# Three of eight one-hot columns of the sorting loop move from VectorE to ScalarE

## The reference

```
edge_index = jnp.stack([src, dst])
x = x + _L0_gnn_ref(_layernorm(x, axis=-1), edge_index, L0_gnn_W, L0_gnn_b)

def _L0_gnn_ref(x, edge_index, W, b):
    ...
    src, dst = (edge_index[0], edge_index[1])
    loop = jnp.arange(n, dtype=src.dtype)
    src = jnp.concatenate([src, loop])
    dst = jnp.concatenate([dst, loop])
    deg = jax.ops.segment_sum(jnp.ones_like(src, dtype=x.dtype), dst, num_segments=n)
    dinv = jnp.where(deg > 0, jax.lax.rsqrt(jnp.maximum(deg, 1e-12)), 0.0)
    norm = dinv[src] * dinv[dst]
    h = x @ W
    msg = h[src] * norm[:, None]
    out = jax.ops.segment_sum(msg, dst, num_segments=n) + b
    return jax.nn.relu(out)
```

## Time and profile before

| what | value |
|---|---|
| median of 3 runs | 3039.4 us (3031.73 to 3045.57) |
| span of the profiled execution, first to last instruction | 2995.2 us |
| median less that span | 44.2 us |
| busy: TensorE | 2491.2 us (83%) |
| busy: VectorE | 1641.0 us (55%) |
| busy: ScalarE | 865.6 us (29%) |
| busy: GpSimd | 587.7 us (20%) |

### The profile page before, as it was taken

The page is one execution under the profiler, slowest core; times in us unless marked ns, Lnnn a source line. Parts: engine busy times, 40 slices in busy tenths (PEclk is TensorE's granted clock), DMA queues, the critical chain, the costliest instruction groups (busy, mean ns, idle before and its releaser), DMA issues. The chain is left out here.

```text
span 2995.2 us, 31395 instructions
## 1 busy us (share of the span) xinstructions
PE 2491.2 (83%) x10830; PEld 1584.9 (53%) x10830; DVE 1641.0 (55%) x3721; ACT 865.6 (29%) x1943; POOL 587.7 (20%) x563
## 2 busy tenths in 40 slices
PE   4877974999957999995568999999999879858987
PEld 1344553999954777773443454444554434534443
DVE  9999435222243889885235897718962442431000
ACT  2165110111111767672111465105631100101110
POOL 0000037354502444530110000000000001012221
PEclk9999975999978899997689999999999989779989
DMA  4000436568643555542433553215533120469996
GB/s 132 0 1 1 143 82 183 191 217 270 216 131 100 157 151 155 153 110 91 144 123 135 197 189 112 78 60 170 167 111 124 54 96 2 168 213 346 347 345 218
DMA packets 195418, 440.43 MB, mean 147 GB/s; under 512 B 25163, under 2 KB 45371, under 8 KB 194782
## 3 DMA queue, kind: packets, MB, share of 16 engines
q1 hardware_dynamic: 156942, 344.67, 34.4%
q0 software_dynamic: 38320, 93.76, 12.0%
HBM read 394.21 MB, written 43.93 MB: 146 GB/s over the span
## 5 line engine op out<-in xcount | busy, mean ns | idle before, releaser
L2177 PE MATMUL psum<-x_res,HH 125*128 125x512 f32 (+1 forms) x960 | 351.9, 526 | 19.8 <-DVE x_res L2367 19.8
L2177 PEld LDWEIGHTS psum<-x_res,HH 125*128 125x128 f32 x960 | 181.4, 193 | 179.5 <-issue 156.5
L1154 POOL DMA_INDIRECT recd<-edge_records,edge_slots x160 | 194.4, 1215 | 327.9 <-issue 321.5
L1521 POOL DMA_INDIRECT hg<-HT,srcidx x196 | 191.4, 976 | 260.1 <-PE psum L1642 129.6
L1683 ACT ACTIVATE hg<-hg,ex 128x129 f32<-128x129 f32 x784 | 235.2, 389 | 1.6
L1642 PE MATMUL psum<-hg,Dh 128*125 128x258 f32 x784 | 208.6, 425 | 6.6 <-DVE ACC L1584 4.0
L2167 PE MATMUL psum<-W,XO 128*125 128x512 f32 x480 | 209.0, 596 | 0.0
L2926 PE MATMUL psum<-wd,XN 128*40 128x512 f32 (+1 forms) x704 | 167.6, 635 | 27.7 <-DMA wd<-in_L_ffn_W_down 27.7
L1642 PEld LDWEIGHTS psum<-hg,Dh 128*125 128x125 f32 x784 | 160.7, 210 | 40.5 <-issue 6.6
L1188 PE MATMUL psum<-xgT,w 128*128 128x192 f32 x1024 | 174.7, 330 | 1.8 <-DMA w<-in_L_ffn_w 1.8
L1188 PEld LDWEIGHTS psum<-xgT,w 128*128 128x128 f32 x1024 | 168.0, 192 | 6.2 <-DMA w<-in_L_ffn_w 3.2
(11 more groups left out here) (507 smaller groups left out, 4041.8 us busy)
## 6 DMA issues: line engine op xcount, KB each, us to landing
wd<-in_L_ffn_W_down SPq DMA_DIRECT2D x30, 2560.0 KB
w<-in_L_ffn_w SPq DMA_DIRECT2D x64, 1024.0 KB, 15.0
MK<-CT SPq DMA_DIRECT2D x80, 625.0 KB, 3.8
wu<-in_L_ffn_W_up SPq DMA_DIRECT2D x8, 2730.0 KB, 19.4
rows<-ROWS POOLq DMA_DIRECT2D x24, 625.0 KB, 7.3
w<-in_L_ffn_W SPq DMA_DIRECT2D x18, 512.0 KB
t<-in_L_ffn_tv_W SPq DMA_DIRECT2D x16, 512.0 KB
targets<-DROW SPq DMA_DIRECT2D x49, 128.0 KB, 3.7
```

The source lines that it names most:

```text
L1154: pool.indirect_dma_start(out=g.recd, out_offset=bass.IndirectOffsetOnAxis(ap=g.posi[:, c:c + 1], axis=0), in_=g.E8[:, c, :], in_offset=No ...
L1521: pool.indirect_dma_start(out=hg[j % RING][:, c, :], out_offset=None, in_=g.HT, in_offset=bass.IndirectOffsetOnAxis(ap=g.srcidx[:, j * CH ...
L2177: return pe.matmul(flat[:, at:at + x1 - x0], HH[:, k, h * DH + c * 128:h * DH + c * 128 + 128], z[n % 4][:, x0:x1], start=(k == 0 and i < ...
```

## The change

In each batch columns 2, 5 and 7 (`BY_ACT`) are left out by VectorE and made by ScalarE in `act_place`. One column is three activations: the distance |iota - hif| into a small buffer `gap` (two of these in turn), a wait for it (`apart`), and two Relus, max(0, value - value x distance), one for the source and one for the target. With integers this is the value where the distance is 0, and 0 elsewhere. The negated factors stand in `less`: -hif and -dnext are made by VectorE (semaphore `negated`), -src by ScalarE from `srci`, which raises `attributes` to two. ScalarE waits for these and for `MADE` ahead of the loop. Its order per tile changes: batch 2k, H row k-1, batch 2k+1, copy of tile k. TensorE waits for a column on the semaphore of the engine that makes it. The ring rule (`sorted_`) holds for both engines.

```diff
--- before.py
+++ after.py
@@ -261,6 +261,8 @@
 
         ge, oh, cum = early(TP, NT + 1, EC), early(TP, NT, EC), early(TP, NT, EC)
         zero, pad, Wt = early(TP, NT, EC), early(128, NB * CH, 8), early(128, KC, D)
+        less = early(TP, 3, EC)
+        gap = early(TP, NB * CH).bitcast(F16).rearrange("p (u n) -> p u n", u=2)
         srci, dsti, ea = s.sb("srci", [TP, EC], I32), s.sb("dsti", [TP, EC], I32), s.sb("ea", [TP, EC, 4])
         E8, dstf = g.E8, s.sb("dstf", [TP, EC])
         tri, none = s.sb("tri", [TP, TP]), s.sb("none", [128, D])
@@ -297,11 +299,14 @@
         sums, taken = s.sig("ct_rows_used"), s.sig("tile_added")
         distance, target_hot = s.sig("risen"), s.sig("rows")
         placed, sorted_, made = s.sig("one_placed"), s.sig("ones_sorted"), s.sig("slots_turned")
+        negated, apart, placed_act = s.sig("scaled_by_act"), s.sig("newmax"), s.sig("rowsT")
         norm = Norm(g, s)
         CTr, MASKr = g.CT.rearrange("(k s) d -> s k d", s=128), g.MASK.rearrange("(k s) d -> s k d", s=128)
         recd_rows = g.recd.rearrange("(p c) k -> p c k", p=128)
         groups = ((0, 4), (4, 8), (8, NT))
         READY, MADE, ONES = 9, 14, 16
+        BY_ACT = (2, 5, 7)
+        BY_DVE = tuple(c for c in range(BATCH) if c not in BY_ACT)
 
         def sp_program():
             sp.dma_start(dsti[:], dst.rearrange("(p c) -> p c", c=EC)).then_inc(*dst_in.up(16))
@@ -371,7 +376,10 @@
 
         def pe_sort(i):
             for c in range(BATCH):
-                pe.wait_ge(*placed.at((2 * BATCH + 1) * i + 2 * c + 3))
+                if c in BY_ACT:
+                    pe.wait_ge(*placed_act.at(len(BY_ACT) * i + BY_ACT.index(c) + 1))
+                else:
+                    pe.wait_ge(*placed.at((2 * len(BY_DVE) + 1) * i + 2 * BY_DVE.index(c) + 3))
                 ins = pe.matmul(g.PS[:, 7, 0:2 * NB * CH], L[i % 2][:, c, :],
                                 R[i % 2][:, c, :, :].rearrange("p k n -> p (k n)"), start=(i + c == 0),
                                 stop=(BATCH * i + c == EC - 1))
@@ -480,6 +488,8 @@
             step(dve.scalar_tensor_tensor(pos[:], lowf[:], float(NB * CH), hif[:], ALU.mult, ALU.add))
             step(dve.tensor_copy(posi[:], pos[:]))
             step(dve.tensor_scalar(dnext[:], E8[:, :, 1], 1.0, None, ALU.add))
+            dve.tensor_scalar(less[:, 0, :], hif[:], -1.0, None, ALU.mult).then_inc(*negated.up())
+            dve.tensor_scalar(less[:, 2, :], dnext[:], -1.0, None, ALU.mult).then_inc(*negated.up())
 
         def dve_edge_terms():
 
@@ -550,7 +560,7 @@
                 dve.wait_ge(*sorted_.at(i - 1))
             dve.tensor_tensor(L[u], g.iota[0:TP, None, 0:128].to_broadcast([TP, BATCH, 128]),
                               lowf[:, cols, None].to_broadcast([TP, BATCH, 128]), ALU.is_equal).then_inc(*placed.up())
-            for c in range(BATCH):
+            for c in BY_DVE:
                 n = BATCH * i + c
                 dve.tensor_scalar(R[u][:, c, 0, :], g.iota[0:TP, 0:NB * CH], hif[:, n:n + 1], E8[:, n, 0:1], ALU.is_equal,
                                   ALU.mult).then_inc(*placed.up())
@@ -560,7 +570,7 @@
         def dve_sort():
 
             norm.dve_statistics()
-            dve.wait_ge(*attributes.at(1))
+            dve.wait_ge(*attributes.at(2))
             dve.wait_ge(*p.at(MADE))
             for k in range(NT):
                 norm.dve_load(k)
@@ -609,17 +619,37 @@
                 act.wait_ge(*mm.at(j - 1))
             act.activation(Dh[j % 2][:], away[:], ACT.Relu, bias=1.0, scale=-1.0).then_inc(*target_hot.up())
 
+        def act_place(i):
+
+            u = i % 2
+            if i >= 2:
+                act.wait_ge(*sorted_.at(i - 1))
+            for c in BY_ACT:
+                n = BATCH * i + c
+                g2 = gap[:, placed_act.count % 2, :]
+                act.activation(g2, g.iota[0:TP, 0:NB * CH], ACT.Abs, bias=less[:, 0, n:n + 1]).then_inc(*apart.up())
+                act.wait_ge(*apart.now())
+                act.activation(R[u][:, c, 0, :], g2, ACT.Relu, bias=E8[:, n, 0:1], scale=less[:, 1, n:n + 1])
+                act.activation(R[u][:, c, 1, :], g2, ACT.Relu, bias=dnext[:, n:n + 1],
+                               scale=less[:, 2, n:n + 1]).then_inc(*placed_act.up())
+
         def act_program():
             act.wait_ge(*src_in.at(32))
             act.activation(E8[:, :, 0], srci[:], ACT.Copy)
+            act.activation(less[:, 1, :], srci[:], ACT.Copy, scale=-1.0).then_inc(*attributes.up())
             act.activation(E8[:, :, 2:6], ea[:], ACT.Copy).then_inc(*attributes.up())
             norm.act_root()
             act.wait_ge(*p.at(READY))
             act.activation(C[:], none[0:TP, None, 0:1].to_broadcast([TP, NT, NW]), ACT.Copy).then_inc(*cleared.up())
+            act.wait_ge(*attributes.at(2))
+            act.wait_ge(*negated.at(2))
+            act.wait_ge(*p.at(MADE))
             for k in range(NT):
-                norm.act_copy(k)
+                act_place(2 * k)
                 if k:
                     act_take(k - 1)
+                act_place(2 * k + 1)
+                norm.act_copy(k)
             act_take(NT - 1)
             act.wait_ge(*made.at(3))
             for j in range(NB):
```

## The result

The changed kernel is a little slower. In 20 runs of each its median is 3043.37 us (3037.56 to 3052.68) against 3036.03 us; the ratio is 1.0027, 95% interval 1.0020 to 1.0034, some 8 us. Both lie inside the 0.5% that the prediction called no change, but clear of zero. The predicted 3041 us lies 2.4 us under the measured 3043.4, inside the range 3030 to 3055; of the change itself 1.9 us were predicted and some 8 measured.

A forecast was written before the change was run, and what follows sets the result against it. VectorE bounds the sorting loop before; the change moves the bound to ScalarE, whose late start eats the gain. Span 2995.2 + 1.9 + 44.2 around it = 3041 us, range 3030 to 3055.

The forecast's parts named there:

- VectorE's part: Sorting loop: three of eight columns leave VectorE, batch 3.55 us, tile 7.56 us; at most 28.8 us gained.
- ScalarE's column: One Abs and two Relus on ScalarE in the sorting loop: 1.404 us a column, 84.2 us over twenty batches.
- two-pointer price: ScalarE activation with bias and scale pointers: 183 ns over a plain copy at 512 elements, so 548 ns at 196.
- the 3x of the Trainium skill: Rule preferring VectorE for relu, max and mul, up to about 3x faster per element; a ScalarE column would be 1.44 us.
- The start: Loop start: ScalarE clears C first and begins its columns at 49.99 us, losing 10 us of head start.
- The middle: ScalarE's H row between batches waits for TensorE's products: 0.27 us a tile, nine times, 2.4 us.
- the slack: Time from a tile's copy until ScalarE comes to the H row, by which products must be over: 4.70 us.
- The second rival: TensorE's clock at 0.50 throughout the products, 6.9 us each, stalling ScalarE 26.5 us: +29 us, 3068 us; chance 7%.
- The end: Loop end: last copy at 145.4 us, then products; last H row at about 150.0 instead of 148.12 us, +1.9 us.
- The total: Whole kernel: profiled span 2995.2 us, plus 1.9 us change, plus 44.2 us taken as lying around the span: 3041 us.
- The signs: Sorting loop: VectorE 70 to 80% busy, ScalarE over 90%, stalls up to 0.7 us, first counting matmul 149 to 154 us.

The follow-up runs named there:

- e8: Changed kernel without ScalarE's columns and their matmuls; only the sorting loop compares: first counting matmul at 125.18 us (single run, 2972.79 us).
- e12: Changed kernel with C cleared early, H rows behind both batches, three and two ScalarE columns in turn, run again; 0.9924 of the kernel before, 3009.21 us.
- e1: Changed kernel with ScalarE's clearing of C moved ahead of its wait for the variance; 0.9976 of the kernel before, 3025.98 us.
- e3: Changed kernel with two idle matmuls ahead of each TensorE wait for a ScalarE column in odd batches; 0.9974 of the kernel before, 3024.54 us.
- e7: Changed kernel with C cleared early, H rows behind both batches, three and two ScalarE columns in turn; 0.9937 of the kernel before, 2980.49 us.

## Why the prediction was right, and where a term was off

**VectorE's part**: right. A batch with five columns was to be 3.55 us; e8's tile of 7.54 us shows it.

**ScalarE's column**: predicted 1.404 us, measured 1.37 (Abs 0.445, Relus 0.551 and 0.536 on the mean). The two-pointer price taken from an unlike shape held within 12 ns. Most of the difference is a slip in reading a row: four L605 of 389 ns in 1.25 us overlap by 0.10 us and not by 0.09, which makes a column 1.384. Over 60 columns the term is off by -1.8 us. The estimate by the 3x of the Trainium skill ("ScalarE: Activation LUTs", "Rules for kernel authors") was 1.44. Measured, a column costs ScalarE 2.9 times what it costs VectorE, but that is three instructions against two; one Relu from start to start takes 0.44 to 0.46 us against 0.24, 1.9 times. So no run here tests the rule's figure, which is per element. It did not decide anything either: e12 gains 23 us by going against the rule, on an engine that was idle.

**The start**: the loss of 10 us was seen and right (VectorE waited 6.87 us for sort 0, up to 55.59; e1 gives the loss back). One part of the step was wrong. The two negations on VectorE were said to be hidden under ScalarE's late start. They come ahead of the variance, for which ScalarE waits before it clears C, so they count: the root starts at 40.13 instead of 39.35, the first Abs at 50.78 instead of 49.99, +0.8 us. Of this the two negations are 0.3 us (both together, not each). VectorE was 0.2 us later before them already, and another 0.3 us is a gap ahead of its statistics, at 33.06, which the kernel before does not have; its cause is not shown. A chain was followed on one engine and not through the wait on the other.

**The middle**: this is the term that was mis-sized. The place, the slack (4.70 us) and the mechanism were named, and the stall was put at 0.27 us a tile on the old share and the old length of slow products. Neither carried over. The mean was 4.11 us then and is 4.88 now. Seven of ten are slow instead of five, and they take 5.3 to 5.6 us where the five took 4.2 to 5.0, because the slow clock now begins at the products and no longer 1 to 2 us ahead of them. The seven stalls, 1.24 to 1.54 us each, make 9.4 us and break the overlap of 0.1 us with the instruction before each time: 10.1 us instead of 2.4, +7.7 us. Six of them stand beside a granted clock of 0.50; the seventh is the first tile's. The second rival said this in its direction and was too strong in size: the clock comes back in the course of the products and three of ten are not hit, so it costs 8 us more than the forecast and not 27. Its weight of 7% was for the whole; a case between the two should have been in the sum.

**The end**: 4.35 us from the last copy to the last H row, against 4.6. In all: start +0.8, columns -1.8, stalls +7.7 and the last stretch -0.3 make +6.4 on the predicted +1.9, and the trace has +8.33.

**The total**: 3041 us came from a span and 44.2 us "around it". What lies around a span is 1.75 us; the rest was the difference in level between the profiled execution and the timed runs. The sum survived only since both were carried unchanged. That 3041 lies so near is luck in part: the three runs it starts from have a median of 3039.4 us and all twenty have 3036.0, so a start 3.4 us too high made up for more than half of what the change was put too low. The difference is what a profile of before can predict here, not the level.

**The signs**: VectorE's share from 60 to 140 us is 73%, as foretold (70 to 80%), and it waits for the sorts. ScalarE's is 88% and not over 90%, the stalls are 1.24 to 1.54 us and not up to 0.7, and the first counting matmul, at 158.95, misses the foretold 149 to 154. All three misses are the middle step.

What was not tried: moving the negations off VectorE's path, and any split finer than five of sixteen columns.

## What to carry to other kernels

Work moved to an idle engine starts when that engine's own list lets it: look at what stands ahead of the first moved instruction, free until then, and move it (11.5 us in e1's trace). In an in-order list, put the instruction that waits for a third engine behind the new work, with slack for that engine's slow case, not for its mean. Then split by price until both engines are full, not by a round number: with both moves three of eight gained 15 us, two of eight 19, and five of sixteen 21 and 23; without them three of eight lost 8.

## What the runs showed of the hardware

TensorE's granted clock fell to 0.50 although no single wait in the tile was longer than 0.87 us; before it fell the engine did matmuls of 0.34 us, one or two at a time, up to 1.4 us apart. With two idle matmuls ahead of each wait in the odd batches (e3) it stood at 1.00 from 60 to 140 us. The eight product matmuls of a tile take 5.3 to 5.4 us where the clock falls at their start, against 3.6 to 3.7 where it stays.

The level of the time changed by 1% from one occasion to another, and nearly all of it shows in a loop that the change does not touch, that of the second graph layer. The first and last start of its 196 VectorE instructions, in the profile of the changed kernel, in that of e7 (on the occasion with a median of 3001.2 us for the kernel before) and in that of e12, which is the kernel of e7 (on the occasion with 3032.1 us):

```profile
L1582 DVE CUSTOM_DVE_ANT_0 junk<-mb,psum x196: 681/684/690, 978.0 to 1391.5; 125x512 f32<-125x512 bf16 x196
```

```profile
L1584 DVE CUSTOM_DVE_ANT_0 junk<-mb,psum x196: 681/683/690, 945.7 to 1324.2; 125x512 f32<-125x512 bf16 x196
```

```profile
L1584 DVE CUSTOM_DVE_ANT_0 junk<-mb,psum x196: 681/684/690, 943.9 to 1351.2; 125x512 f32<-125x512 bf16 x196
```

The same instructions span 413.5, 378.5 and 407.3 us, while each of them takes the same 0.68 us. e7 and e12 are one kernel on one chip number, so a difference between chips is not what these rows show. What they do show is where the time goes: ahead of these instructions VectorE waits 37.1 us in all in the first profile and 30.3 in the third, and the profile gives as releaser only "remote", not an instruction of this core. e7 has no such wait. What stands behind it is not shown.
